# First attention of a gated cross-attention layer pair: the values' low parts as a third accumulated product instead of a VectorE sum

## The chip, the cores and the metric

The kernel runs on one core of a Trainium2 chip. The metric is device time in microseconds (us) of one execution. The engines named here are TensorE (PE; its weight loads are listed apart as PEld), VectorE (DVE), ScalarE (ACT), GpSimd (POOL) and SyncE (SP).

## The reference

Batch B = 32, sequence S = 128, width D = 128, context of C = 77 rows. Four sublayers follow one another, each added to the residual stream with a gate of tanh. The one that matters here is the first:

```python
# H = 16 heads, D_K = 8
qh = einsum('bsd,hdk->hbsk', layernorm(x), W_q);  kh, vh = the same of ctx with W_k, W_v
attn = softmax(qh @ kh^T / sqrt(D_K))
out = einsum('hbst,hbtk->hbsk', attn, vh)         # heads side by side: 128 columns
x = x + tanh(g_xattn[0]) * (out @ W_o.T + b_o)
```

After it come a quantised feed-forward layer with a convolution, a second attention (16 heads of 64) and a mixture of eight experts.

## The kernel before, in words

Values that need more than 16-bit precision are held as a high and a low half in fp16, and a product of two of them is made of three products, high by high, low by high and high by low, accumulated in PSUM.

The first attention is the function `attention0`. `project0` has left the scaled queries and keys in `qst` and `kst`, and the values in `vals`, of shape [C, B, H, 2, 9]: for each batch and head the eight high parts and a 1, then the eight low parts and a 0. The column of ones makes each product also give the sum of the probabilities.

The work is cut into 128 units, n = 0 to 127: batch b = n // 4, and four of the 16 heads each. Units go in pairs, and two pairs are one batch: an even pair and an odd pair. The order on each engine is written out by hand:

- TensorE, for each pair: `scores` of the next pair (line 619), by query, only for the maxima; `scores_by_key` (lines 630 and 634), the scores transposed with the negated maxima added by a product with the identity; `mix_values` of the pair two back (lines 646 and 647), probabilities by values; then, in an even pair, `turn` of the batch two back (line 654), a transpose of the normalised heads, and, in an odd pair, `project` (line 659), the three products with the output weights.
- ScalarE, for each unit: two exponentials of the same scores, `probs` in fp32 (line 688) and `probs_h` in fp16 (line 689); once a batch, after the third unit, `turned_h` (line 693).
- GpSimd, for each unit: `probs_l` = `probs` − `probs_h` (line 610).
- VectorE: in an even pair `residual` of the batch three back (line 725), the maxima of the next pair's two units (line 706), `statistics` (729), `normalise` of the batch two back (lines 710, 712, 716), `aggregate` (733); in an odd pair the two maxima and `out_low` (line 721), which makes `turned_l`.

In `mix_values` each head has a region of 18 columns in bank 6: `probs_h` by all 18 columns of `vals` (line 646), then `probs_l` by the nine high columns, accumulated onto the first nine (line 647). `normalise` adds the two nines with a reduce into `summed` (line 710, semaphore `totalled`), takes the reciprocal of the ninth column (712, `inverted`) and multiplies (716, `normed`). The mix of the next batch overwrites bank 6, so the first mix of a batch waits for `totalled` (line 643); the turn waits for `normed` (line 651). The loop over the 64 pairs is unrolled; behind it stand the mixes of the last two pairs and the turn and projection of the last two batches.

Of the kernel before, what the change touches and what calls it, by code (L numbers as in the profile page):

```python
# [9 lines left out]
ALU = mybir.AluOpType  # L10
ACT = mybir.ActivationFunctionType
AX = mybir.AxisListType

B, S, D = 32, 128, 128
C = 77
H = 16
DK0 = D // H
# [553 lines left out]
def attention0(nc, w, bank, qst, kst, vals):  # L571
# [3 lines left out]
    with Memory(nc, "attention0") as m:  # L575
        PAIRS = B * G // 2
        SLOTS = 8
# [1 line left out]
        negmax = m.sb("negmax", [S, G, HG], FP16)  # L579
        probs = m.sb("probs", [C, 2, HG, S])  # L580
        probs_h, probs_l = m.sb("probs_h", [C, SLOTS, HG, S], FP16), m.sb("probs_l", [C, SLOTS, HG, S], FP16)
        summed, recip, heads_out = m.sb("summed", [S, H, DK0 + 1]), m.sb("recip", [S, H]), m.sb("heads_out", [S, H, DK0])
        turned_h, turned_l = m.sb("turned_h", [D, S], FP16), m.sb("turned_l", [D, S], FP16)
        bn = m.sb("bn", [S, 2, 6])
        (scored, maxed, shifted, exped, p_split, mixed, totalled, inverted, normed, turned, ot_hi, ot_lo, projected, added,
         bn_done) = (
            m.sem(n) for n in ("scored", "maxed", "shifted", "exped", "p_split", "mixed", "totalled", "inverted", "normed",
                               "turned", "ot_hi", "ot_lo", "projected", "added", "bn_done"))
        block = m.block()
        score = [bank[i][:, 0:HG * C].rearrange("p (h c) -> p h c", c=C) for i in range(2)]  # L590
        score_t = [bank[2 + i][0:C, :].rearrange("p (h s) -> p h s", s=S) for i in range(4)]
        mix = bank[6][:, 0:H * 2 * (DK0 + 1)].rearrange("p (h i k) -> p h i k", i=2, k=DK0 + 1)
        out_t, out_p = bank[7][:, 0:S], bank[7][:, S:S + D]

        def units(pair):

            return (2 * pair, 2 * pair + 1)

        def rows(n):

            j = n % G
            return slice(32 * j, 32 * j + 32)

        @block.gpsimd
        def _(pool):
            for n in range(B * G):
                pool.wait_ge(exped, n + 1)
                if n >= SLOTS:
                    pool.wait_ge(mixed, n - SLOTS + 1)
                pool.tensor_tensor(probs_l[:, n % SLOTS], probs[:, n % 2], probs_h[:, n % SLOTS], ALU.subtract).then_inc(p_split, 1)  # L610

        @block.tensor
        def _(pe):
            def scores(pair):
                if pair:
                    pe.wait_ge(maxed, 2 * pair)
                for i in range(HG):
                    for n in units(pair):
                        ins = pe.matmul(score[n % 2][:, i], qst[rows(n), i, n // G, :], kst[rows(n), i, n // G, :],
                                        start=True, stop=True)  # L620
                        if i == HG - 1:
                            ins.then_inc(scored, 1)

            def scores_by_key(pair):
                pe.wait_ge(maxed, 2 * pair + 2)
                if pair >= 2:
                    pe.wait_ge(exped, 2 * pair - 2)
                for i in range(HG):
                    for n in units(pair):
                        pe.matmul(score_t[n % 4][:, i], kst[rows(n), i, n // G, :], qst[rows(n), i, n // G, :],  # L630
                                  start=i == 0, stop=False)
                for n in units(pair):
                    for i in range(HG):
                        last = pe.matmul(score_t[n % 4][:, i], negmax[:, n % G, i:i + 1].broadcast_to([S, C]), w.identh[:],  # L634
                                         start=False, stop=i == HG - 1)
                    last.then_inc(shifted, 1)

            def mix_values(pair):
                for n in units(pair):
                    b, j = n // G, n % G  # L640
                    pe.wait_ge(p_split, n + 1)
                    if j == 0 and b:
                        pe.wait_ge(totalled, b)
                    for i in range(HG):
                        v = HG * j + i
                        pe.matmul(mix[:, v], probs_h[:, n % SLOTS, i], vals[:, b, v], start=True, stop=False)
                        last = pe.matmul(mix[:, v, 0], probs_l[:, n % SLOTS, i], vals[:, b, v, 0], start=False, stop=True)
                    last.then_inc(mixed, 1)

            def turn(b):  # L650
                pe.wait_ge(normed, b + 1)
                if b:
                    pe.wait_ge(added, b)
                pe.transpose(out_t, heads_out[:].rearrange("p h k -> p (h k)"), w.ident[:]).then_inc(turned, 1)

            def project(b):
                pe.wait_ge(ot_lo, b + 1)
                for k, (x, wt) in enumerate(((turned_h, w.o0h), (turned_h, w.o0l), (turned_l, w.o0h))):
                    last = pe.matmul(out_p, x[:], wt[:, 0, :], start=k == 0, stop=k == 2)
                last.then_inc(projected, 1)  # L660

            scores(0)
            for pair in range(PAIRS):
                if pair + 1 < PAIRS:
                    scores(pair + 1)
                scores_by_key(pair)
                if pair >= LAG:
                    mix_values(pair - LAG)
                b = pair // 2 - 2
                if b >= 0 and pair % 2 == 0:  # L670
                    turn(b)
                if b >= 0 and pair % 2 == 1:
                    project(b)
            for pair in range(PAIRS - LAG, PAIRS):
                mix_values(pair)
            for b in range(B - 2, B):
                turn(b)
                project(b)
# [23 lines left out]
        @block.vector  # L702
        def _(dve):
            def maximum(n):
                dve.wait_ge(scored, n + 1)
                dve.tensor_reduce(negmax[:, n % G], score[n % 2], AX.X, ALU.max, negate=True).then_inc(maxed, 1)

            def normalise(b):
                dve.wait_ge(mixed, (b + 1) * G)
                dve.tensor_reduce(summed[:], mix.rearrange("p h i k -> p h k i"), AX.X, ALU.add).then_inc(totalled, 1)  # L710
                dve.wait_ge(totalled, b + 1)
                dve.reciprocal(recip[:], summed[:, :, DK0]).then_inc(inverted, 1)
                dve.wait_ge(inverted, b + 1)
                if b:
                    dve.wait_ge(turned, b)
                dve.tensor_tensor(heads_out[:], summed[:, :, 0:DK0], recip[:].unsqueeze(2).broadcast_to([S, H, DK0]),
                                  ALU.mult).then_inc(normed, 1)

            def out_low(b):
                dve.wait_ge(ot_hi, b + 1)  # L720
                dve.tensor_tensor(turned_l[:], out_t, turned_h[:], ALU.subtract).then_inc(ot_lo, 1)

            def residual(b):
                dve.wait_ge(projected, b + 1)
                dve.scalar_tensor_tensor(w.X[:, b, :], out_p, w.tg0[:], w.X[:, b, :], ALU.mult, ALU.add).then_inc(added, 1)

            def statistics(b):
                dve.wait_ge(added, b + 1)
                dve.bn_stats(bn[:, b % 2], w.X[:, b]).then_inc(bn_done, 1)

            def aggregate(b):
                dve.wait_ge(bn_done, b + 1)
                dve.bn_aggr(w.mv[:, b], bn[:, b % 2])

            maximum(0)
            maximum(1)
            for pair in range(PAIRS):
                b, first = pair // 2, pair % 2 == 0
                if first and b >= 3:
                    residual(b - 3)  # L740
                for n in units(pair + 1):
                    if n < B * G:
                        maximum(n)
                if first and b >= 3:
                    statistics(b - 3)
                if first and b >= 2:
                    normalise(b - 2)
                if first and b >= 3:
                    aggregate(b - 3)
                if not first and b >= 2:  # L750
                    out_low(b - 2)
            residual(B - 3)
            statistics(B - 3)
            aggregate(B - 3)
            for b in range(B - 2, B):
                normalise(b)
                out_low(b)
                residual(b)
                statistics(b)
                aggregate(b)  # L760
# [1120 lines left out]
```

## Time and profile before

| | |
|---|---|
| median of 3 runs | 1517.34 us (1514.23 to 1517.55) |
| the profiled execution's own time | 1511.63 us |
| its span, first to last instruction | 1509.8 us |
| TensorE busy | 1249.5 us (83%) |
| VectorE busy | 1207.7 us (80%) |
| mean granted TensorE clock | 0.882 |
| first to last product of the first attention | 134.39 to 341.3 us |

The profile is that of one execution. Busy time of TensorE is modelled: its matmuls are pipelined, so several lie over one another, and the distance from one start to the next says more of the pace than the duration of one. The granted clock is a share of 2.4 GHz: 0.50 is 1.2 GHz. A view that gives "[0.37 <-DVE ...]" behind an instruction means that its engine was idle for 0.37 us just before it, and which instruction of which engine ended that.

### The profile page before, as it was taken

Reading aid. Unit: us, or ns where it says so; the run is one execution under the profiler, and the core shown is the slowest. Engines: PE = TensorE matmul, PEld = TensorE weight load, DVE = VectorE, ACT = ScalarE, POOL = GpSimd, SP = SyncE. Lnnn points to the kernel's source line nnn. Section 1 sums busy time; section 2 is a strip of 40 time slices with the busy share of each in tenths; the row PEclk is TensorE's granted clock in tenths of the full one; section 3 lists DMA queues with packets and bytes.
Section 4 is the critical chain, followed back from the end, with each engine's and each line's share of the span. In section 5 each row is a group of like instructions: output and inputs, shape, how many; then the busy total and the mean of one; then the engine's idle time right before and its main releaser. Section 6 shows DMA issues by size and latency. Waiting matters only on the chain. (4 is left out here: it accounts for less than half of the span.)

```text
span 1509.8 us, 42427 instructions
## 1 busy us (share of the span) xinstructions
PE 1249.5 (83%) x15029; PEld 938.4 (62%) x15029; DVE 1207.7 (80%) x3230; ACT 923.4 (61%) x1858; POOL 801.6 (53%) x831
## 2 busy tenths in 40 slices
PE   1588888876994599999999999999998388888887
PEld 1445666653663377777777777877777245555555
DVE  4987555555998778888888888888888589988996
ACT  0678666653663477777777777777766244555554
POOL 1243777762215355455555455555545257777778
PEclk9678555557996699999999999999999599999999
DMA  9000000000000000000000000000000000000000
GB/s 240 24 1 1 2 2 2 2 2 1 1 1 1 1 2 1 0 0 0 0 0 0 0 0 0 0 0 0 0 0 1 0 2 8 8 7 7 7 7 15
DMA packets 24076, 13.06 MB, mean 9 GB/s; under 512 B 8596, under 2 KB 22332, under 8 KB 23996
## 3 DMA queue, kind: packets, MB, share of 16 engines
q1 hardware_dynamic: 12955, 8.60, 2.2%
q10 hardware_dynamic: 11040, 3.42, 1.0%
q8 instruction: 47, 0.77, 0.2%
q14 instruction: 34, 0.27, 0.1%
HBM read 9.92 MB, written 2.10 MB: 8 GB/s over the span
## 5 line engine op out<-in xcount | busy, mean ns | idle before, releaser
L1166 POOL TENSOR_TENSOR attention_pl_l<-attention_probs_l,attention_ph_l 128x512 f16<-128x512 f32 x128 | 148.0, 1156 | 202.1 <-ACT attention_ph_l L1323 202.1
L610 POOL TENSOR_TENSOR attention_probs_l<-attention_probs,attention_probs_h 77x512 f16<-77x512 f32 x128 | 145.4, 1151 | 94.0 <-ACT attention_probs_h L689 62.8
L1570 POOL TENSOR_TENSOR mixture_hidden_l<-mixture_hidden,mixture_hidden_h 128x512 f16<-128x512 f32 x128 | 148.2, 1158 | 75.0 <-ACT mixture_hidden_h L1657 75.0
L1166 POOL TENSOR_TENSOR attention_pl_c<-attention_probs_c,attention_ph_c 77x512 f16<-77x512 f32 x128 | 148.5, 1160 | 28.9 <-ACT attention_ph_c L1330 28.9
L1385 DVE TENSOR_REDUCE attention_negmax<-bank 128x2 f16<-128x410 f32 x256 | 137.3, 578 | 24.8 <-PE bank L1218 22.3
L1666 ACT ACTIVATE mixture_tanh<-bank 128x512 f32<-128x512 f32 x128 | 76.4, 597 | 105.5 <-PE bank L1617 105.5
L1323 ACT ACTIVATE attention_probs_l<-bank 128x512 f32<-128x512 f32 x128 | 76.4, 597 | 99.0 <-PE bank L1233 99.0
L1229 PE MATMUL bank<-attention_th,attention_keys 128*128 128x512 f16 (+1 forms) x256 | 96.9, 378 | 41.8 <-issue 41.6
L1615 PE MATMUL bank<-mixture_xs,moeh 128*128 128x512 f16 x256 | 98.2, 383 | 31.9 <-DVE mixture_hidden L1748 31.9
L1200 PE MATMUL bank<-attention_keys,ah 128*128 128x128 f16 x1024 | 108.7, 221 | 12.0 <-DVE attention_keys L1414 11.8
L1233 PEld LDWEIGHTS bank<-identh,attention_negmax 128*128 128x128 f16 (+1 forms) x1024 | 83.2, 107 | 55.8
L688 ACT ACTIVATE attention_probs<-bank 77x512 f32<-77x512 f32 x128 | 75.9, 593 | 64.7 <-PE bank L634 63.6
L1200 PE MATMUL bank<-v1h,attention_keys 128*128 128x256 f16 (+1 forms) x512 | 105.7, 274 | 1.3 <-DVE attention_vl_c L1392 1.3
L1740 DVE SCALAR_TENSOR_TENSOR mixture_half<-mixture_tanh,bank 128x512 f32<-128x512 f32 x128 | 87.2, 682 | 15.7 <-ACT mixture_tanh L1666 15.7
L1233 PE MATMUL bank<-identh,attention_negmax 128*128 128x128 f16 (+1 forms) x1024 | 98.9, 219 | 0.0
L1616 PE MATMUL bank<-mixture_xs,moel 128*128 128x512 f16 x256 | 97.8, 382 | 0.0
L1617 PE MATMUL bank<-mixture_xs,moeh 128*128 128x512 f16 x256 | 97.6, 381 | 0.0
L1249 PE MATMUL bank<-attention_vh_l,attention_ph_l 128*128 128x65 f16 x512 | 95.5, 194 | 2.0 <-POOL attention_pl_c L1166 2.0
L1231 PE MATMUL bank<-attention_tl,attention_keys 128*128 128x512 f16 (+1 forms) x256 | 97.0, 379 | 0.0
L1230 PE MATMUL bank<-attention_th,attention_keys 128*128 128x512 f16 (+1 forms) x256 | 96.9, 379 | 0.0
L1249 PE MATMUL bank<-attention_vl_l,attention_ph_l 128*128 128x65 f16 x512 | 95.7, 192 | 0.0
L1249 PE MATMUL bank<-attention_vh_c,attention_ph_c 77*128 77x65 f16 x512 | 95.6, 195 | 0.0
(331 smaller groups left out, 4950.6 us busy)
## 6 DMA issues: line engine op xcount, KB each, us to landing
X<-in_x SPq DMA_DIRECT2D x4, 512.0 KB, 9.4
out<-X SPq DMA_DIRECT2D x8, 256.0 KB, 2.3
ctx<-in_ctx SPq DMA_DIRECT2D x1, 1232.0 KB
setup_nat_w<-in_w SPq DMA_DIRECT2D x1, 1024.0 KB, 14.4
setup_nat_f<-in_fw ACTq DMA_DIRECT2D x2, 256.0 KB, 7.0
setup_nat_q<-in_q ACTq DMA_DIRECT2D x1, 512.0 KB, 8.1
setup_nat_k<-in_kv ACTq DMA_DIRECT2D x1, 512.0 KB, 8.9
setup_nat_v<-in_kv ACTq DMA_DIRECT2D x1, 512.0 KB, 10.3
```

The source lines that it names most:

```text
L610: pool.tensor_tensor(probs_l[:, n % SLOTS], probs[:, n % 2], probs_h[:, n % SLOTS], ALU.subtract).then_inc(p_split, 1)
L1166: last = pool.tensor_tensor(low[:, g % 2], whole[:, g % 2], high[:, g % 2], ALU.subtract)
L1200: last = pe.matmul(dst, x, y, start=i == 0, stop=i == 2)
L1229: pe.matmul(dst, kh, th[:, g], start=True, stop=False)
L1231: pe.matmul(dst, kh, tl[:, g], start=False, stop=False)
L1233: last = pe.matmul(dst[:, h], negmax[:, g, h:h + 1].broadcast_to([S, width]), w.identh[:], start=False, stop=h == HG - 1)
L1249: last = pe.matmul(mix[:, h], x, y, start=i == 0, stop=i == len(products) - 1)
L1385: last = dve.tensor_reduce(negmax[:, g, 2 * i:2 * i + 2], score[i], AX.X, ALU.max, negate=True)
L1570: pool.tensor_tensor(hidden_l[:, e % 4, j], hidden[:, e % 2, j], hidden_h[:, e % 4, j], ALU.subtract).then_inc(hid_lo, 1)
L1615: pe.matmul(dst, wh, xs[:, u, 0], start=True, stop=False)
L1616: pe.matmul(dst, wl, xs[:, u, 0], start=False, stop=False)
L1617: last = pe.matmul(dst, wh, xs[:, u, 1], start=False, stop=True)
```

## The change

Each head's region of bank 6 shrinks from 18 to 9 columns. In place of one product of 18 columns and one of 9, three products of 9 columns are accumulated into the same nine: `probs_h` by the high values, `probs_h` by the low values, `probs_l` by the high values. The reduce and its tile `summed` and semaphore `totalled` go; reciprocal and multiplication read bank 6 themselves. The first mix of a batch waits for `normed`, the end of the multiplication, in place of `totalled`.

```diff
-        mix = bank[6][:, 0:H * 2 * (DK0 + 1)].rearrange("p (h i k) -> p h i k", i=2, k=DK0 + 1)
+        mix = bank[6][:, 0:H * (DK0 + 1)].rearrange("p (h k) -> p h k", k=DK0 + 1)
...
                     pe.wait_ge(p_split, n + 1)
                     if j == 0 and b:
-                        pe.wait_ge(totalled, b)
+                        pe.wait_ge(normed, b)
                     for i in range(HG):
                         v = HG * j + i
-                        pe.matmul(mix[:, v], probs_h[:, n % SLOTS, i], vals[:, b, v], start=True, stop=False)
-                        last = pe.matmul(mix[:, v, 0], probs_l[:, n % SLOTS, i], vals[:, b, v, 0], start=False, stop=True)
+                        pe.matmul(mix[:, v], probs_h[:, n % SLOTS, i], vals[:, b, v, 0], start=True, stop=False)
+                        pe.matmul(mix[:, v], probs_h[:, n % SLOTS, i], vals[:, b, v, 1], start=False, stop=False)
+                        last = pe.matmul(mix[:, v], probs_l[:, n % SLOTS, i], vals[:, b, v, 0], start=False, stop=True)
                     last.then_inc(mixed, 1)
...
                 dve.wait_ge(mixed, (b + 1) * G)
-                dve.tensor_reduce(summed[:], mix.rearrange("p h i k -> p h k i"), AX.X, ALU.add).then_inc(totalled, 1)
-                dve.wait_ge(totalled, b + 1)
-                dve.reciprocal(recip[:], summed[:, :, DK0]).then_inc(inverted, 1)
+                dve.reciprocal(recip[:], mix[:, :, DK0]).then_inc(inverted, 1)
                 dve.wait_ge(inverted, b + 1)
                 if b:
                     dve.wait_ge(turned, b)
-                dve.tensor_tensor(heads_out[:], summed[:, :, 0:DK0], recip[:].unsqueeze(2).broadcast_to([S, H, DK0]),
+                dve.tensor_tensor(heads_out[:], mix[:, :, 0:DK0], recip[:].unsqueeze(2).broadcast_to([S, H, DK0]),
                                   ALU.mult).then_inc(normed, 1)
```

## Rows read from the trace of the kernel before

**Rows 1.** The page: busy time of each engine, and the span in 40 slices, tenths.

```profile
PE 1249.5 (83%) x15029; PEld 938.4 (62%) x15029; DVE 1207.7 (80%) x3230; ACT 923.4 (61%) x1858; POOL 801.6 (53%) x831
...
PE   1588888876994599999999999999998388888887
...
PEclk9678555557996699999999999999999599999999
```

**Rows 2.** The table by windows: start, end, length, then busy time of PE, PEld, DVE, ACT, POOL, granted clock.

```profile
150.66:333.23 182.57, 148.06 (x2426) 117.52 (x2426) 102.45 (x317) 122.80 (x262) 131.28 (x117) 0.50 0.01 2
```

**Rows 3.** The timeline (start us, duration us, instruction): line 710, 28 batches apart.

```profile
152.12 0.44 DVE L710 TENSOR_REDUCE attention_summed<-bank 128x144 f32<-128x288 f32 x1
...
328.84 0.44 DVE L710 TENSOR_REDUCE attention_summed<-bank 128x144 f32<-128x288 f32 x1
```

**Rows 4.** The waits from 150 to 330 us: total, times, longest.

```profile
PE bank L659 <- DVE attention_turned_l L721: 24.4, 29, 1.4
...
PE bank L646 <- DVE attention_summed L710: 10.7, 29, 0.4
```

**Rows 5.** The timeline of one even pair, its TensorE and VectorE instructions.

```profile
232.72 0.24 PE L619 MATMUL bank<-layer_kst,layer_qst 32*128 32x77 f16 x2
...
232.83 0.35 DVE L725 SCALAR_TENSOR_TENSOR X<-bank,tg,X 128x128 f32<-128x128 f32 x1 [0.60 <-PE bank L659]
...
233.20 0.86 DVE L706 TENSOR_REDUCE attention_negmax<-bank 128x4 f16<-128x308 f32 x2
...
233.32 1.07 PE L634 MATMUL bank<-identh,attention_negmax 128*77 128x128 f16 x8
...
234.18 0.44 DVE L710 TENSOR_REDUCE attention_summed<-bank 128x144 f32<-128x288 f32 x1
...
234.65 0.25 DVE L712 RECIPROCAL attention_recip<-attention_summed 128x16 f32<-128x16 f32 x1
234.73 0.10 PEld L646 LDWEIGHTS bank<-layer_vals,attention_probs_h 77*128 77x128 f16 x1 [0.56 <-POOL attention_probs_l L610]
234.76 0.17 PE L646 MATMUL bank<-layer_vals,attention_probs_h 77*128 77x18 f16 x1 [0.37 <-DVE attention_summed L710]
...
234.94 0.29 DVE L716 TENSOR_TENSOR attention_heads_out<-attention_summed,attention_recip 128x128 f32<-128x128 f32 x1
...
235.16 0.17 PE L647 MATMUL bank<-layer_vals,attention_probs_l 77*128 77x9 f16 x1
235.28 0.18 PEld L654 LDWEIGHTS bank<-ident,attention_heads_out 128*128 128x128 f32 x1
```

**Rows 6.** The timeline of the odd pair behind it, up to the next pair.

```profile
235.69 0.25 PE L619 MATMUL bank<-layer_kst,layer_qst 32*128 32x77 f16 x2
...
236.97 0.59 ACT L688 ACTIVATE attention_probs<-bank 77x512 f32<-77x512 f32 x1 [0.92 <-PE bank L634]
...
237.60 0.17 PE L647 MATMUL bank<-layer_vals,attention_probs_l 77*128 77x9 f16 x1
237.94 0.27 ACT L693 ACTIVATE attention_turned_h<-bank 128x128 f16<-128x128 f32 x1
...
238.24 0.29 DVE L721 TENSOR_TENSOR attention_turned_l<-bank,attention_turned_h 128x128 f16<-128x128 f32 x1 [1.22 <-ACT attention_turned_h L693]
...
238.59 0.29 PE L659 MATMUL bank<-o0h,attention_turned_h 128*128 128x128 f16 x1 [0.82 <-DVE attention_turned_l L721]
...
239.03 0.25 PE L619 MATMUL bank<-layer_kst,layer_qst 32*128 32x77 f16 x2
```

**Rows 7.** The timeline behind the loop: last product of the last mix, first turn.

```profile
335.98 0.17 PE L647 MATMUL bank<-layer_vals,attention_probs_l 77*128 77x9 f16 x1
335.98 0.18 PEld L654 LDWEIGHTS bank<-ident,attention_heads_out 128*128 128x128 f32 x1
```

**Rows 8.** Groups by line from 140 to 340 us: two of the projection's loads.

```profile
L659 PEld LDWEIGHTS bank<-o0l,attention_turned_h 128*128 128x128 f16 x31 | 3.7, 118 | 0.0
L659 PEld LDWEIGHTS bank<-o0h,attention_turned_h 128*128 128x128 f16 x31 | 3.3, 105 | 28.8 <-DVE attention_turned_l L721 28.8
```

More of the change, by code:

```diff
@@ L581, in attention0 @@
         probs_h, probs_l = m.sb("probs_h", [C, SLOTS, HG, S], FP16), m.sb("probs_l", [C, SLOTS, HG, S], FP16)
-        summed, recip, heads_out = m.sb("summed", [S, H, DK0 + 1]), m.sb("recip", [S, H]), m.sb("heads_out", [S, H, DK0])
+        recip, heads_out = m.sb("recip", [S, H]), m.sb("heads_out", [S, H, DK0])
         turned_h, turned_l = m.sb("turned_h", [D, S], FP16), m.sb("turned_l", [D, S], FP16)
         bn = m.sb("bn", [S, 2, 6])
-        (scored, maxed, shifted, exped, p_split, mixed, totalled, inverted, normed, turned, ot_hi, ot_lo, projected, added,
+        (scored, maxed, shifted, exped, p_split, mixed, inverted, normed, turned, ot_hi, ot_lo, projected, added,
          bn_done) = (
-            m.sem(n) for n in ("scored", "maxed", "shifted", "exped", "p_split", "mixed", "totalled", "inverted", "normed",
+            m.sem(n) for n in ("scored", "maxed", "shifted", "exped", "p_split", "mixed", "inverted", "normed",
                                "turned", "ot_hi", "ot_lo", "projected", "added", "bn_done"))
```

## The prediction, made before the change was run

> **What bounds the kernel now.** I began with the page. TensorE is busy for 83% of the span, VectorE for 80%, and the granted clock falls to half in five of the forty slices [rows 1]. Those slices are the first attention, the only stage that the change touches. The table by windows of that stage confirms it: in 182.57 us TensorE is busy 148.06 and VectorE 102.45, at a granted clock of 0.50, that is 1.2 GHz [rows 2]. So VectorE is only 56% busy in this stage, and its 80% belongs to other stages. A sum taken off VectorE is worth something only where somebody waits for it.
>
> Next, how regular the stage is. The reduce of line 710 starts at 152.12 us and, 28 batches later, at 328.84 [rows 3]: (328.84 − 152.12) / 28 = 6.31 us per batch. One batch can therefore stand for all, and the sum is one batch's difference times a count.
>
> Then the waits. TensorE waits for the reduce of line 710 29 times, 10.7 us in all, 0.37 each; it waits for `turned_l` (line 721) 24.4 us in all [rows 4]. Both waits are real and lie in different halves of a batch. In the timeline of one batch the reader should see two closed chains.
>
> The even pair runs from 232.72 to 235.69, 2.97 us [rows 5, 6]. The residual of line 725 on VectorE is released by the projection's end, then come two maxima, the statistics, the reduce (234.18 to 234.62), and only then TensorE's first load of the mix at 234.73. Sixteen products follow, the first at 234.76 and the last at 235.16, then the turn at 235.28 and the next pair. TensorE's own products ahead of the mix (line 634, eight from 233.32 in 1.07 us) are over at 234.39; VectorE's chain ends last ahead of the mix.
>
> The odd pair runs from 235.69 to 239.03, 3.34 us [rows 6]. Scores, then ScalarE's exponentials at 236.97, its `turned_h` at 237.94, VectorE's `turned_l` at 238.24, the projection at 238.59. The mix of this half lies beside ScalarE's work: its last product starts at 237.60, and TensorE is then idle for 0.82 us until the projection.
>
> **The change, part by part.** The reduce, its 0.44 us and the 0.03 behind it go, 32 times: 14.1 us of VectorE's busy time by 32 × 0.44 [rows 5]. Nothing of that is credited as such; only what it does to TensorE's next start counts.
>
> *The wait that replaces it.* TensorE's mix must now wait for the multiplication of line 716 (`normed`), because that is the last reader of the bank. In the new order the reciprocal starts where the reduce did, 234.18. From the start of the reciprocal to that of the multiplication is 0.29 us (234.65 to 234.94), and the multiplication takes 0.29 [rows 5]. It ends at 234.18 + 0.29 + 0.29 = 234.76, where the reduce ended at 234.62: 0.14 later. That the two now read PSUM instead of SBUF I cost at nothing: line 721 reads 128 columns of PSUM in 0.29 us [rows 6], and line 716 the same number from SBUF in 0.29 [rows 5]. The reciprocal shows no PSUM case, so its bound above is +0.06, and for the multiplication too: 0.35 of line 725 is the longest operation on 128 columns in the chain [rows 5]. The bound below is nothing, since the same elements are worked on. The handoff from VectorE's end to the mix's first load is 0.11 now (234.62 to 234.73), while that from the multiplication to the turn is 0.05 (235.23 to 235.28) [rows 5]. I take 0.11, since the waiting instruction stays the same one, and keep 0.05 as the other end. Start of the mix: **+0.14** (ends +0.08 and +0.26).
>
> *The third product.* Each head gets three products in place of two, 24 for 16 in a pair. The moving columns don't change, 18 + 9 against 3 × 9. Starts lie (235.16 − 234.76) / 15 = 0.0267 us apart [rows 5], with 18 and 9 columns alternating, so the pace is not set by the columns: making the wide product narrow saves nothing. Two products with the same stationary operand each load it: the projection has one load of `turned_h` with `o0h` and one with `o0l` [rows 8]. So eight products more are 8 × 0.0267 = **+0.21** in the even pair. In the odd pair they are 0.21 inside an idle time of 0.82: nothing, with 0.61 of cover left; without that cover it would be 0.21 there too.
>
> A single load lasts 0.10 us in the rows, yet the next one starts 0.027 later [rows 5]. The Trainium skill (TensorE: Matmul & The Clock Gate, LDWEIGHTS) gives a load as its columns over 1.2, so 107 ns for 128 columns, and elsewhere on that page a fast load in a quarter of the cycles; priced by the first, eight loads would be 0.86 us. The trace agrees with the first as a duration (0.10) and with the second as a pace (0.027), and the pace goes into the sum.
>
> *The turn.* Today it is held back by the multiplication: that ends at 235.23, the turn's load starts at 235.28, 0.12 after the last product started [rows 5]. Where nothing holds it, behind the loop, the turn's load starts in the same hundredth as the last product, 335.98 [rows 7]. In the new order the multiplication is over before the mix begins, so the turn follows at once: **−0.12**. What is late next is the mix itself.
>
> *Sum.* +0.14 + 0.21 − 0.12 = +0.23 us per batch. Nothing behind it absorbs this: the odd pair's chain starts from TensorE's scores, and ScalarE and GpSimd wait for them. Queued behind the new wait on TensorE are the mix, the turn and the next pair's scores; their consumers shift by the same 0.23. Times 29, the times that the old wait occurs [rows 4]: +6.7 us. The first batches run without projection and I give them nothing. Behind the loop one reduce fewer lies bare (−0.47), the two last mixes are 16 products longer (+0.43) and start 0.14 later: +0.1. In all **+6.8 us**.
>
> The profiled run took 1511.63 us for a span of 1509.8; the change makes it 1518.4. The median shown is 1517.34, 0.4% above that run, so I forecast 1517.3 + 6.8 = **1524.1 us**, 0.45% slower. About 0.3% (4.6 us) is what a measurement of this kernel can tell from no change.
>
> **The rivals.**
>
> *Short handoff, no visible difference.* With 0.05 from multiplication to mix the batch costs +0.17: 29 × 0.17 + 0.1 = +5.0, 1522.3. That is 0.33%, and the three runs shown spread over 3.3 us, so it may well read as no change. For it: 0.05 and 0.06 are seen behind the multiplication and behind line 721 (238.53 to 238.59) [rows 5, 6]. Against it: the mix's own first load shows 0.11. Chance 0.16.
>
> *The third product is no product.* If the array found its weights in place for the second product of a head, the extra load would cost nothing, and the batch +0.14 − 0.12 = +0.02: 29 × 0.02, less 0.33 behind the loop, is +0.3, 1517.6. Against it stand the two loads of one tile in the projection [rows 8]. Chance 0.08.
>
> *Loads at full length.* If the eight added loads did not overlap, each would cost its 0.10 us [rows 5]: +0.8 in the even pair, just hidden by 0.82 in the odd one. 29 × (0.80 + 0.02) + 1.3 = +25, 1542. Against it: sixteen loads of the same shape pass at 0.027 today. Chance 0.03.
>
> *The clock comes up, faster than before.* The stage runs at half clock throughout, while TensorE is busy 148.06 of 182.57 us [rows 2], and stages with full digits of TensorE run near full clock [rows 1]. If the added work lifted the stage to 2.4 GHz, the stretches paced by the array would shrink: 1.28 us from scores to exponentials, 0.44 of projection, 0.41 of turn [rows 5, 6], and the mix of 24 × 0.027 = 0.64, 2.8 us in all, of which latencies keep a part; a saving of 0.7 to 1.4 us, say 1.0, for 29 batches. 1524 − 29 = 1495. It decides as soon as the stage's clock reads above 0.5 for most of it. The Trainium skill (TensorE: Matmul & The Clock Gate, What's actually happening) says that the throttled state is the default and that activity releases it, which by itself would favour this case; the trace has TensorE 81% busy through the whole stage at half clock, and the change adds loads but not one moving column. Chance 0.04.
>
> **How the numbers follow.** Forecast 0.69, short handoff 0.16, no product 0.08, full-length loads 0.03, clock 0.04. Slower by over 0.3%: 0.69 + 0.03 = 0.72. Within 0.3%: 0.16 + 0.08 = 0.24. Faster: 0.04. The range takes in the ends of the handoff (+5.0) and of both PSUM reads (29 × 0.35 + 0.1 = +10.3), and about two us of the runs' spread on either side: 1519 to 1530. Left out are the no-product case, the clock and the full-length loads, 0.15 together.
>
> **What would show it.** Right: the reduces of line 710's kind 6.54 us apart (now reciprocals); no reduce between statistics and reciprocal; the mix's first load in the even pair some 2.15 us after the pair's start, where it was 2.01 (232.72 to 234.73), released by the multiplication; 24 loads 0.027 apart; the turn in step with the last product; TensorE's idle time before the projection down from 0.82 to about 0.6; clock 0.50. The odd pair stays at 3.34 and the even one goes from 2.97 to 3.20. Wrong: a period at or below 6.31; a gap between the products other than 0.027; a reciprocal or multiplication that grows on PSUM; a clock above 0.50 in the stage; or a change in a later stage, where the text gives none.

## The result and the profile after

| | before | after |
|---|---|---|
| median of the runs | 1515.88 us (4 runs) | 1528.25 us (4 runs, 1526.89 to 1531.55) |
| span of the profiled execution | 1509.8 us | 1525.1 us |
| first attention, first score product to last `aggregate` | 134.4 to 342.0: 207.6 us | 132.9 to 347.3: 214.4 us |
| mixture, first to last product of its first line | 1207.9 to 1496.1: 288.2 us | 1215.5 to 1511.3: 295.8 us |

The ratio is 1.0085, interval 1.0063 to 1.0107: slower by 12.4 us between the medians, 12.9 by the ratio. The forecast was +6.8. In the profiled executions the stage that was changed took that: 214.4 − 207.6 = 6.8. The rest came in a stage of which the prediction expected nothing. First the stage that was forecast. Of the changed kernel, the timeline of an even pair, to be laid beside [rows 5]; the mix's three products now stand on lines 646 to 648, and the lines of the turn and the projection are one higher:

```profile
234.15 0.31 PE L660 MATMUL bank<-o0h,attention_turned_l 128*128 128x128 f16 x1
...
234.40 0.24 PE L619 MATMUL bank<-layer_kst,layer_qst 32*128 32x77 f16 x2
...
234.50 0.35 DVE L724 SCALAR_TENSOR_TENSOR X<-bank,tg,X 128x128 f32<-128x128 f32 x1 [0.60 <-PE bank L660]
...
234.87 0.86 DVE L707 TENSOR_REDUCE attention_negmax<-bank 128x4 f16<-128x308 f32 x2
...
235.65 0.28 DVE L728 BATCH_NORM_STATS2 attention_bn<-X 128x6 f32<-128x128 f32 x1
...
235.85 0.24 DVE L711 RECIPROCAL attention_recip<-bank 128x16 f32<-128x16 f32 x1
236.12 0.29 DVE L715 TENSOR_TENSOR attention_heads_out<-bank,attention_recip 128x128 f32<-128x128 f32 x1
...
236.53 0.10 PEld L646 LDWEIGHTS bank<-layer_vals,attention_probs_h 77*128 77x128 f16 x1 [0.69 <-POOL attention_probs_l L610]
236.56 0.17 PE L646 MATMUL bank<-layer_vals,attention_probs_h 77*128 77x9 f16 x1 [0.49 <-DVE attention_heads_out L715]
236.56 0.10 PEld L647 LDWEIGHTS bank<-layer_vals,attention_probs_h 77*128 77x128 f16 x1
236.59 0.17 PE L647 MATMUL bank<-layer_vals,attention_probs_h 77*128 77x9 f16 x1
236.59 0.10 PEld L648 LDWEIGHTS bank<-layer_vals,attention_probs_l 77*128 77x128 f16 x1
236.62 0.17 PE L648 MATMUL bank<-layer_vals,attention_probs_l 77*128 77x9 f16 x1
...
237.18 0.17 PE L648 MATMUL bank<-layer_vals,attention_probs_l 77*128 77x9 f16 x1
237.18 0.18 PEld L655 LDWEIGHTS bank<-ident,attention_heads_out 128*128 128x128 f32 x1
...
237.59 0.25 PE L619 MATMUL bank<-layer_kst,layer_qst 32*128 32x77 f16 x2
```

Read it from the top: reciprocal straight behind the statistics, multiplication over at 236.41, the mix's first load at 236.53. `probs_h` is loaded twice in a row, 0.03 us apart, for lines 646 and 647. The 24th product starts at 237.18, and the turn's load in the same hundredth. The pair takes 237.59 − 234.40 = 3.19 us. In the odd pair behind it, TensorE's idle time ahead of the projection has shrunk from 0.82 us [rows 6] to 0.61:

```profile
240.49 0.29 PE L660 MATMUL bank<-o0h,attention_turned_h 128*128 128x128 f16 x1 [0.61 <-DVE attention_turned_l L720]
```

The waits of the stage, from 150 to 340 us, answer to [rows 4]; each is again counted 29 times:

```profile
PEld bank L646 <- POOL attention_probs_l L610: 20.1, 29, 0.7
PE bank L660 <- DVE attention_turned_l L720: 17.7, 29, 0.6
...
PE bank L646 <- DVE attention_heads_out L715: 14.3, 29, 0.5
```

The wait was not removed but exchanged, 14.3 us for 10.7. The wait on `turned_l` sank from 24.4 to 17.7: the odd pair's extra products lie in it. (The row that names GpSimd is the same wait seen from the load: GpSimd's unit had long been done.)

Now the page, with its instruction queues. First the kernel before, then the changed one:

```profile
q8 instruction: 47, 0.77, 0.2%
q14 instruction: 34, 0.27, 0.1%
```

```profile
PE 1261.7 (83%) x15541; PEld 950.0 (62%) x15541; DVE 1195.1 (78%) x3198; ACT 923.2 (61%) x1858; POOL 802.3 (53%) x831
...
PEclk9787555557996699999999999999999599999999
...
q8 instruction: 51, 0.84, 0.2%
q14 instruction: 42, 0.34, 0.1%
```

VectorE has 32 instructions fewer and 12.6 us less work, and the whole is slower. The queue q14, which carries code, moved eight packets more for a shorter VectorE stream. That is the track to the rest. VectorE in the mixture, where its loop jumps back to its head, in the kernel before:

```profile
1321.18 0.19 DVE L1733 TENSOR_TENSOR mixture_weight<-mixture_is 128x32 f32<-128x32 f32 x1
1321.83 0.69 DVE L1758 TENSOR_TENSOR mixture_part<-bank,mixture_weight 128x512 f32<-128x512 f32 x1 [0.45 <-issue]
```

and in the changed one, where the second jump looks the same:

```profile
1329.18 0.19 DVE L1732 TENSOR_TENSOR mixture_weight<-mixture_is 128x32 f32<-128x32 f32 x1
1332.29 0.69 DVE L1757 TENSOR_TENSOR mixture_part<-bank,mixture_weight 128x512 f32<-128x512 f32 x1 [2.91 <-POOL X L1564]
...
1410.19 0.69 DVE L1757 TENSOR_TENSOR mixture_part<-bank,mixture_weight 128x512 f32<-128x512 f32 x1 [2.88 <-POOL X L1564]
```

VectorE's idle time at the jump is 0.45 us before and 2.9 after; "issue" means that the engine waited for nothing that the profile shows. The releaser named in the changed kernel, GpSimd's line 1564, is a guess of the view: the addition that this instruction has to wait for began at 1325.67 and took 1.27, so it had been done for five us. The loop runs three times and so jumps back twice. GpSimd's additions around the first jump, one per expert, show the price with its echo: 7.62 us apart here (1330.68 to 1338.30) where the same step took 5.12 before, and 5.60 apart in the next step where it had been 4.04, because TensorE stood idle for 2.75 us and its next products then run at half clock (granted 0.50 from 1336 to 1339 us): 0.63 us instead of 0.38.

```profile
1334.44 0.39 PE L1614 MATMUL bank<-mixture_xs,moeh 128*128 128x512 f16 x1 [2.75 <-DVE mixture_hidden L1747]
...
1336.25 0.63 PE L1615 MATMUL bank<-mixture_xs,moel 128*128 128x512 f16 x1
```

The second jump costs 2.45 us (7.54 against 5.09), without the echo. Together 2.5 + 1.6 + 2.45 = 6.5 of the mixture's 7.6 us.

The other 1.05 us are three smaller delays that come with the stalls. Halfway through each of the three passes, where the second chunk of a pass begins, the step between two of GpSimd's additions is 5.00 us where it was 4.65, and VectorE's row there shows 0.33 us of idle time. This is the row of the first pass, first in the kernel before, then in the changed one:

```profile
1284.84 0.69 DVE L1758 TENSOR_TENSOR mixture_part<-bank,mixture_weight 128x512 f32<-128x512 f32 x1
1292.84 0.69 DVE L1757 TENSOR_TENSOR mixture_part<-bank,mixture_weight 128x512 f32<-128x512 f32 x1 [0.33 <-issue]
```

No jump lies there. The delay appears in exactly the kernels that also stall at the jumps. All other steps are equal to 0.02 us, so the mixture's surplus is accounted for.

The account of the span, +15.3: −1.5 ahead of the first attention, +6.8 in it, −0.1 to the end of the feed-forward products, +2.4 from there to the mixture, +7.6 in the mixture, the rest is rounding. The −1.5 and the +2.4 I leave without a cause: from first to last product of line 1200, the second attention takes 645.3 us before and between 643.9 and 648.6 in the eight other kernels, without an order in it.

### The profile page after: what moved, and what is told of

Read it like the earlier page. It is cut to its first block and busy times, and to the rows that moved or that the text cites. A ratio compares the mean times of both kernels' runs of the same rounds, so it can differ in the third digit from the quotient of the medians.

```text
span 1525.1 us, 43419 instructions
## 1 busy us (share of the span) xinstructions
PE 1261.7 (83%) x15541; PEld 950.0 (62%) x15541; DVE 1195.1 (78%) x3198; ACT 923.2 (61%) x1858; POOL 802.3 (53%) x831
## 5 line engine op out<-in xcount | busy, mean ns | idle before, releaser
L707 DVE TENSOR_REDUCE attention_negmax<-bank 128x4 f16<-128x308 f32 x128 | 55.3, 474 | 51.7 <-PE bank L619 51.2
```

## The experiments

The theory for the stage was the prediction's own. For the mixture: VectorE's loop lies elsewhere against the blocks in which code is fetched, since 32 instructions ahead of it are gone; rivals are TensorE's 512 extra products (and as many loads), and chance.

**VectorE's stream given its length back.** The changed kernel with one instruction more per batch:

```diff
+        spare = m.sb("spare", [S, 4])
...
             def out_low(b):
+                for i in range(1):
+                    dve.memset(spare[:, i:i + 1], 0.0)
                 dve.wait_ge(ot_hi, b + 1)
```

> The changed kernel with one tiny memset on VectorE per batch in front of out_low, where VectorE is idle for 1.22 us: 32 instructions of a few hundredths of a us, so that VectorE's instruction stream behind the first attention is as long as before the change. Theory (code position): in the changed kernel the mixture stage is 7.6 us longer because VectorE's loop there lies elsewhere against the blocks in which its code is fetched, and it stands still twice for 2.9 us at the jump back. With the 32 instructions given back both stalls go, the mixture is as long as before (288 us from first to last product), and the whole is only the first attention's +6.8 us, ratio 1.004 to before. Rival (TensorE's 512 extra instructions, or chance): both stalls stay, ratio 1.0085.

Measured: 1520.52 us (6 runs) against 1515.7, ratio 1.0037, interval 1.0017 to 1.0057. The period is 6.53 as in the changed kernel, the mixture takes 288.3 us, before 288.2. The jump back:

```profile
1331.64 0.19 DVE L1735 TENSOR_TENSOR mixture_weight<-mixture_is 128x32 f32<-128x32 f32 x1
1332.29 0.69 DVE L1760 TENSOR_TENSOR mixture_part<-bank,mixture_weight 128x512 f32<-128x512 f32 x1 [0.45 <-issue]
```

The stalls are gone, with TensorE's stream as long as in the changed kernel. 32 instructions more make the kernel faster: each measured against before, 1.0037 in place of 1.0085, 7 us, and the two intervals do not touch.

**The stall without the change.** The kernel before, with `range(3)` in the same place, 96 instructions more:

> The kernel before, arithmetic untouched, with three tiny memsets on VectorE per batch in front of out_low: 96 instructions. Theory (code position, in blocks of 128 instructions, as 8 KB packets of 64-byte instructions suggest): 96 more is the same position as 32 fewer, so the two stalls of 2.9 us appear in the mixture of a kernel without the change, and the whole is 6 to 8 us longer, ratio 1.005; the first attention keeps its period of 6.31 us. Rival (the stalls need the change's own instructions): ratio 1.000 and no stall. If stalls appear in another number, the block is of another size.

Measured: 1520.83 us (6 runs), ratio 1.0036, interval 1.0013 to 1.0058; period 6.31; mixture 297.4 us. Its two jumps:

```profile
1323.19 0.69 DVE L1761 TENSOR_TENSOR mixture_part<-bank,mixture_weight 128x512 f32<-128x512 f32 x1 [2.92 <-POOL X L1568]
...
1401.08 0.69 DVE L1761 TENSOR_TENSOR mixture_part<-bank,mixture_weight 128x512 f32<-128x512 f32 x1 [2.89 <-POOL X L1568]
```

The stalls appear in a kernel whose arithmetic is that of before, at both jumps. The profiled execution's span is 7.7 us longer than that of before (1517.5 to 1509.8): +9.1 in the mixture and −1.4 in all that lies ahead of it, the latter within the scatter named above. The 9.1 are more than the changed kernel's 7.6 because here TensorE's clock fell to half behind both stalls. The medians are 5.1 us apart.

**A whole block more.** `range(4)`, 128 instructions:

> The kernel before with four tiny memsets per batch on VectorE, 128 instructions. Theory (blocks of 128 instructions): the loop of the mixture lies where it lay before, so there is no stall at the jumps back, the mixture takes 288 us, and the count of instruction packets on the second instruction queue is near 34, not 43. Rival (any longer stream brings the stalls, or another block size): stalls of 2.9 us, mixture near 297 us.

Measured, one run: 1516.45 us. Mixture 288.2 us, 35 packets on q14, and the jump:

```profile
1326.67 0.69 DVE L1761 TENSOR_TENSOR mixture_part<-bank,mixture_weight 128x512 f32<-128x512 f32 x1 [0.43 <-issue]
```

So −32 and +96 stall, 0 and +128 do not: what counts is the position of the loop, and not the length of the stream. The four positions fit a period of 128 instructions. They would fit one of 64 as well; for 128 speaks only the size of the packets. In the stretch from 1290 to 1420 us, which holds both jumps, q14 carries 2 packets in the kernels without the stall and 10 or 11 in those with it. The packets themselves give the size: 0.27 MB in 34 packets is 8 KB, and q8, which grew by 0.07 MB for TensorE's 1,024 extra instructions (512 products and 512 loads), gives some 64 bytes for one: about 128 to a packet of q14.

The Trainium skill (Runtime: NRT & Kernel Launch, Instruction fetch mechanics) says that code is prefetched in order, in blocks of 256 instructions of which two are held, and that a taken branch to a target outside the blocks held must wait for a DMA. The trace agrees with the mechanism, 2.9 us for a jump against 0.45, with more packets of code behind it. It does not agree with the size for VectorE. The loop has 296 VectorE instructions in the built program. If the two blocks of 256 are that of the jump and the one before it, the loop stalls only where it starts in the last 39 places of a block; −32 and +96 lie 128 places apart, so both could not stall. If they are that of the jump and the next one, it would stall at 0 and +128 too. What size and number of blocks is right, no run here settles.

**The third product alone.** The kernel before, reduce and wait kept, the 18 columns written by two products:

```diff
-                        pe.matmul(mix[:, v], probs_h[:, n % SLOTS, i], vals[:, b, v], start=True, stop=False)
+                        pe.matmul(mix[:, v, 1], probs_h[:, n % SLOTS, i], vals[:, b, v, 1], start=True, stop=True)
+                        pe.matmul(mix[:, v, 0], probs_h[:, n % SLOTS, i], vals[:, b, v, 0], start=True, stop=False)
```

> The kernel before with the third product alone: 18 columns as before, written by products of 9, 9 and 9 columns, the reduce and its wait kept. Theory (the pace is one weight load, 0.027 us): mix of the even pair 0.64 instead of 0.43 us, of which 0.12 is what the turn waited for the multiplication anyway, so the period goes from 6.31 to 6.40, the whole is 2.7 us longer, ratio 1.002, and no stall in the mixture, as VectorE's stream is unchanged while TensorE's is that of the changed kernel. Rival (no load for the second product): period 6.31. Rival (TensorE's stream causes the stalls): mixture 7 us longer.

Measured: period 6.40 to 6.41, whole ratio 1.0019, interval 0.9998 to 1.0041, so the whole alone would not tell it from no change; the period does. The mixture shows no stall (0.45 and 0.42 us at the jumps). A product without a load of its own is refuted, and so is TensorE's stream as the cause of the stalls.

**The exchanged wait alone.** The changed kernel with one line out, so that the result lacks the values' low parts:

```diff
-                        pe.matmul(mix[:, v], probs_h[:, n % SLOTS, i], vals[:, b, v, 1], start=False, stop=False)
```

> The changed kernel without the product of probs_h by the low values, so the values' low parts are left out of the result. Two products of 9 columns per head, reduce gone, wait on the multiplication. Theory: mix starts 0.14 later than before, lasts 0.43, the turn follows at once, so the period is 6.31 + 0.14 - 0.12 = 6.33, first attention +0.6 us; the two stalls in the mixture stay, because VectorE's stream is that of the changed kernel: whole +7 to +8, ratio 1.005. Rival (the replaced wait is dearer, and the third product free): period near 6.53. Rival (stalls from TensorE's stream): ratio 1.000.

Measured: period 6.32, 1521.41 us, ratio 1.0042, interval 1.0021 to 1.0063, mixture 296.2 us. Both stalls are there with TensorE's old count of instructions. Exchanging the wait costs 0.01 us a batch, the third product alone 0.09, both together 0.22. The difference, 0.12, is the turn's slack: each part alone can spend it, both together only once.

**Who is waited for, moved away.** If TensorE's even pair waits for nothing but VectorE's chain, the remedy is not less VectorE work but VectorE work elsewhere. `normalise` goes to the end of the odd pair, behind `out_low` (in the changed kernel with the one memset per batch of the first experiment):

```diff
-                if first and b >= 2:
-                    normalise(b - 2)
                 if first and b >= 3:
                     aggregate(b - 3)
                 if not first and b >= 2:
                     out_low(b - 2)
+                if not first and b >= 1:
+                    normalise(b - 1)
...
             for b in range(B - 2, B):
-                normalise(b)
+                if b == B - 1:
+                    normalise(b)
```

> The changed kernel, with VectorE's normalise moved from the even pair, behind the maxima and statistics, to the end of the odd pair before it, behind out_low; plus one tiny memset per batch that keeps the code position of before. Theory (TensorE's even pair waits for VectorE's chain and for nothing else): the multiplication is over before the even pair's scores are, TensorE no longer waits ahead of the mix, the even pair becomes TensorE's own work: 1.36 us to the first load of the mix as in the odd pair, 0.11, 24 products 0.64, turn 0.41, that is 2.52 instead of 3.20 us. Period 5.86, first attention 19 us shorter than with the change and 13 shorter than before, no stall in the mixture, ratio 0.991. Rival (ScalarE or GpSimd, busy 5.06 and 4.6 us of a batch, or the odd pair's chain take over): period above 6.1.

> The same move in the kernel before, with its reduce and its two products. Theory: the even pair is TensorE's own work here too and is 0.21 shorter, as the mix has 16 products: 2.31 us, period 5.65, first attention 19 us shorter than before, ratio 0.987; the reduce's 0.44 us now lies where nobody waits, so the old arithmetic is faster than the new one by 6 us. Rival (the reduce delays the residual and the maxima behind it, and ScalarE is nearly full at 5.06 us of 5.65): period near 5.86 and no difference to the other kernel, or the new arithmetic ahead.

Measured, new arithmetic: 1498.97 us against 1514.29 (6 and 11 runs), ratio 0.9905, interval 0.9888 to 0.9922; period 5.88. Old arithmetic: 1495.16 us, ratio 0.9880, interval 0.9858 to 0.9901; period 5.72 to 5.73. Both beat the kernel before and the changed one. The even pair of the new arithmetic (232.98 to 235.52) is TensorE's own 2.54 us:

```profile
232.98 0.24 PE L620 MATMUL bank<-layer_kst,layer_qst 32*128 32x77 f16 x2
...
234.45 0.22 PE L647 MATMUL bank<-layer_vals,attention_probs_h 77*128 77x9 f16 x1
...
235.13 0.45 PE L656 MATMUL bank<-ident,attention_heads_out 128*128 128x128 f32 x1
...
235.52 0.24 PE L620 MATMUL bank<-layer_kst,layer_qst 32*128 32x77 f16 x2
```

No idle time stands ahead of the mix any more. The old arithmetic's batch is 0.08 us longer than its forecast of 5.65. Its even pair takes 2.33 us (236.00 to 238.33) where 2.31 was forecast; its odd pair takes 3.40 instead of 3.34:

```profile
232.60 0.24 PE L619 MATMUL bank<-layer_kst,layer_qst 32*128 32x77 f16 x2
...
232.71 4.78 POOL L610 TENSOR_TENSOR attention_probs_l<-attention_probs,attention_probs_h 77x512 f16<-77x512 f32 x4 [0.94 <-ACT attention_probs_h L689]
...
233.94 0.59 ACT L688 ACTIVATE attention_probs<-bank 77x512 f32<-77x512 f32 x1 [0.34 <-PE bank L634]
```

GpSimd now runs four units without a gap, 4.78 us. ScalarE's exponential of 233.94 would be ready 1.28 us behind the pair's start, 233.88, by [rows 6], but by the code it may overwrite its tile only when GpSimd's first of the four is done, about 233.9. This reading of the last 0.06 us was not tested by itself. The period of the old arithmetic is 0.15 below that of the new; the intervals of the whole, 0.9858 to 0.9901 and 0.9888 to 0.9922, overlap.

## Why the prediction was right in one stage and short in the whole

- **The bound.** Right. VectorE's chain ended last ahead of the mix, and moving it away took 0.65 us off the batch. One reading beside it was wrong: six slices, not five, stand at half clock in [rows 1], and the sixth is the start of the mixture.
- **The replaced wait, +0.14.** In the changed kernel the first load stands 2.13 us behind the pair's start, where it was 2.01 [rows 5]: +0.12. Reciprocal and multiplication were not slower on PSUM: 0.24 and 0.29. The handoff was 0.12, the end that I took; the short one, 0.05, did not come.
- **The third product, +0.21.** 236.56 to 237.18 for 24 starts is 0.027 each, +0.22 for the eight more. In the odd pair it was free: the idle time ahead of the projection sank from 0.82 to 0.61, as forecast.
- **The turn, −0.12.** It starts with the last product. Confirmed as a slack that is spent once by the two experiments with one part each.
- **Sum.** Forecast +0.23 per batch, measured 6.53 − 6.31 = 0.22; stage forecast +6.8, measured +6.8. That the stage came out to the tenth is in part luck: the 29 steady batches gave 6.45 where 6.7 was forecast, the first batches and the part behind the loop gave +0.33 where +0.1 was. Granted clock 0.50 throughout the stage, so the clock's case did not occur, nor did full-length loads.
- **What was short.** The step that failed is a term that the sum does not have: all later stages stand at nothing, without a reason given, and by the prediction's own sign ("a change in a later stage, where the text gives none") it was wrong there. I priced the removed instructions by the time in which they are executed, and nowhere by the place that they hold in VectorE's stream. That place cost +7.6 us in the mixture, more than the whole forecast. The range of 1519 to 1530 held 1528.25 by luck: what made it reach so far up, slower PSUM reads, did not come, and the cost that did come was not among its ends. (Its lower end also lies 1.3 us below what the text adds up, 1522.3 less two.)
- **Old against new.** By the period, the old arithmetic is the better one here once the wait is gone: its reduce lies where nobody waits, while the third product lies on TensorE.

## What to carry to other kernels

Ask of each removed operation who waits behind it, and what becomes the release in its place: here 0.44 us went off VectorE and TensorE was released 0.12 later, because the bank came free behind a longer chain of shorter steps. If an engine's chain is waited for in one half of a period and idle in the other, move it before you shorten it: that took the changed kernel's first attention from 214.4 to 194.1 us, where the shortening had made it 6.8 longer. And after any change of the number of instructions ahead of a loop, look at that loop's jumps back and at the packets of the code queues before you credit or blame the change: here 32 instructions were worth 7 us in a stage 900 us later.

## What was not expected of the hardware

- At a jump back of this loop VectorE is idle for 0.39 to 0.45 us or for 2.9 (3.0 and 3.1 in the kernel without the low product), by the position of the loop: 0 and +128 instructions quiet, −32 and +96 not. With the stalls go 8 to 9 packets more on q14, and 0.35 us more halfway through each pass.
- After such a stall TensorE's granted clock can fall to half, and the next products took 0.63 us instead of 0.38; of the two stalls in the changed kernel, the first did this and the second did not; with 96 instructions more both did, in the kernel without the low product only the second. The length of TensorE's idle time does not decide it: the clock stayed at 1.00 behind 2.98 us of it in the kernel without the low product, and fell behind 2.73 in that with 96 more.
